# A four-layer kernel on one core: the next batch's gated-attention front moved to a round's end, score and one-hot products issued by row groups in turn, and two residual sums made on TensorE

## What is computed

```
x = layernorm(x + gated_attention(x))        # "a": silu(normed @ W_h) gives v and gate, groups of 32 tokens
                                             #      quad_out + lin_out, times gate, @ W_out + b_out + x
x = layernorm(x + experts(x))                # "a": softmax of 8 logits, top 2 of 8 experts
x = layernorm(x + linear_attention(x))       # "b": 16 heads of 8, softmax feature maps, causal sums
x = layernorm(x + product_keys(x))           # "peer": 8 heads; per head the best 8 of 32 + 32 keys, the best 8 sums,
                                             #      those rows of down and up:
    hmid = sigmoid(score) * gelu(x . down[index]);  out = sum(hmid * up[index])
```

## Time and profile before

| | |
|---|---|
| median of 3 runs | 570.6 us |
| the profiled execution | 572.47 us |
| its span, first to last instruction | 570.7 us |
| mean granted TensorE clock | 0.733 of full speed |
| busy: PE, PE weight loads, DVE, ACT, GpSimd (POOL) | 419.4, 300.4, 481.5, 307.2, 182.2 us |
| layers, peer | 0 to 314.3 us, 314.3 to 570.7 us |

### The profile page before, as it was taken

How to read it: one execution, slowest core, us unless ns; L and a number is a source line. 1 busy time by engine, 2 the same in 40 slices (tenths; PEclk the granted TensorE clock), 3 DMA queues, 4 the chain that set the end, 5 groups by cost and what they waited for, 6 DMA issues and landing times. The chain is left out here.

```text
span 570.7 us, 12499 instructions
## 1 busy us (share of the span) xinstructions
PE 419.4 (73%) x4564; PEld 300.4 (53%) x4564; DVE 481.5 (84%) x2076; ACT 307.2 (54%) x639; POOL 182.2 (32%) x208
## 2 busy tenths in 40 slices
PE   1777869987999879965754864756698869784485
PEld 1454547654776457633653323554465555554475
DVE  4485877699887989599894699999999999999991
ACT  0611275426652475313640558483788778786591
POOL 4540122943277143833350330303040404030000
PEclk9997979688867977795555785575757575757577
DMA  7220000000000000000000000000000000000000
GB/s 214 71 59 0 1 2 2 1 2 0 1 1 3 0 2 1 2 1 0 1 2 1 1 1 1 3 1 11 2 11 1 12 2 12 1 11 2 11 2 20
DMA packets 12459, 6.72 MB, mean 12 GB/s; under 512 B 3182, under 2 KB 11758, under 8 KB 12398
## 3 DMA queue, kind: packets, MB, share of 16 engines
q1 hardware_dynamic: 10566, 4.34, 2.8%
q10 hardware_dynamic: 1832, 1.58, 0.9%
HBM read 4.87 MB, written 1.05 MB: 10 GB/s over the span
## 5 line engine op out<-in xcount | busy, mean ns | idle before, releaser
L1746 ACT ACTIVATE hot_last<-iota_f,lo_last 128x128 f16<-128x128 f32 x256 | 77.5, 393 | 0.3 <-DVE lo_last L1872 0.3
L2015 PE MATMUL psum<-hot_w,hot_lo 128*128 128x16 f16 x1536 | 44.3, 174 | 25.1 <-DVE hot_lo L1889 17.9
L2015 PEld LDWEIGHTS psum<-hot_w,hot_lo 128*128 128x128 f16 x1536 | 43.4, 104 | 36.8 <-DVE hot_lo L1889 24.5
L1979 PE MATMUL psum<-x3t,down_t 128*128 128x512 f32 x64 | 45.3, 832 | 16.8 <-ACT hid L1711 15.1
L1889 DVE TENSOR_TENSOR hot_lo<-lo_t,iota_lo 128x4096 f16<-128x4096 f16 x24 | 53.6, 2287 | 0.3
L1659 POOL TENSOR_TENSOR eq<-eq,side_f 128x1024 f16<-128x1024 f16 x14 | 28.9, 2085 | 55.9 <-DVE eq L1850 55.9
L1329 PE MATMUL psum<-q_hi,k_t 32*128 32x128 f16 x256 | 36.1, 259 | 8.9 <-DVE masked L905 7.7
L1667 POOL TENSOR_TENSOR rstd<-rstd,minus_half 128x2 f32<-128x2 f32 x8 | 5.6, 702 | 113.4 <-DVE rstd L1922 113.4
L1819 DVE FIND_INDEX8 side_i<-side,keysims 128x8 uint32<-128x32 f32 x256 | 41.5, 184 | 0.0
L1250 PE MATMUL psum<-we,x1t 128*128 128x512 f32 x64 | 40.2, 777 | 0.4 <-DVE z L842 0.4
L2029 PE MATMUL psum<-upw,mix 128*128 128x128 f32 x256 | 36.9, 306 | 0.0
(11 more groups left out here) (271 smaller groups left out, 1166.8 us busy)
## 6 DMA issues: line engine op xcount, KB each, us to landing
xall<-in_L_attn_x SPq DMA_DIRECT2D x4, 256.0 KB, 6.3
out<-o SPq DMA_DIRECT2D x8, 128.0 KB, 2.3
we<-in_L_ffn_We SPq DMA_DIRECT2D x1, 512.0 KB, 4.4
downn<-in_L_ffn_down SPq DMA_DIRECT2D x1, 512.0 KB, 5.3
upw<-in_L_ffn_up SPq DMA_DIRECT2D x1, 512.0 KB, 6.3
wh<-in_L_attn_W_h SPq DMA_DIRECT2D x1, 256.0 KB, 4.7
keysn<-in_L_ffn_keys_p ACTq DMA_DIRECT2D x1, 256.0 KB, 9.7
wqkv<-in_L_attn_w_qkv ACTq DMA_DIRECT2D x1, 192.0 KB
```

The source lines that it names most:

```text
L1746: ins = nc.scalar.activation(hot_last[:, lane], iota_f[:], ACT.Abs, bias=lo_last[:, lane:lane + 1], scale=-1.0)
L1979: nc.tensor.matmul(bank[H_BANK(b, c)][:], v.down_t[:, c, :], v.x3t[:, N * b:N * b + N], start=True, stop=True).then_inc(h_mm.h, 1)
L2015: ins = nc.tensor.matmul(bank[2 + q][:, c:c + 2 * EH], low, hot_w[:, i, lane // 2, :, :, lane % 2].rearrange("p t e -> p (t e)"), start=(i ...
```

## The change

- `a_qk`, `a_gate`, `a_val` of batch a + 1 are issued at the end of round s on PE, and their Silus there on ACT (`a_front`), in the order qk, gate 0, val 0, val 1, gate 1 (`a_rest` is the last four on PE); batch 1's before round 1. The steps behind them stand elsewhere in the round.
- `b_scores` issues the products of the groups in turn (as many groups as there are banks) and waits once for all of their banks. In rounds 1 to 3 `a_experts(a, 1)` is cut in two between scores.
- `a_z` and `b_z3` on DVE are gone: PE adds the residual to the same PSUM columns as a product with the identity, and mean, variance and normalising read PSUM.
- POOL no longer waits for x1 before the low parts of the scores.
- `hot_w` loses the zero halves: each tile of the pair is a product on its own 64 rows, 8 columns, into a bank of its own; two tiles in turn. `weigh` waits for two quarters at a time. The division by `WEIGHT_SCALE` moves from `weigh` into `upw`, once, on POOL; the memset of `hot_w` is gone.
- `key_scores(0)` is issued before `hidden(0, 1)`.

```
-                for s in range(1, B + 1):
+                a_qk(1)
+                a_rest(1)
+                for s in range(1, B + 1):
...
                 for u in range(T):
                     for c in range(EC):
-                        ins = nc.tensor.matmul(bank[3]..., gated_t, v.wout0, start=(c == 0), stop=(c == EC - 1))
+                        nc.tensor.matmul(bank[3]..., gated_t, v.wout0, start=(c == 0), stop=False)
+                    if u == 0:
+                        wait(pe, xres_ok, b)
+                    ins = nc.tensor.matmul(bank[3]..., ident[:], v.xall[:, T * b + u, :], start=False, stop=True)
...
-                    b_scores(b, 0)
+                    b_scores(b, 0, (0,))
+                    b_scores(b, 0, (1,))
...
                         a_experts(a, 0)
-                        a_experts(a, 1)
                         b_scores(b, 2, (1,))
+                        a_experts(a, 1, (0,))
                         b_scores(b, 3, (0,))
+                        a_experts(a, 1, (1,))
+                        b_scores(b, 3, (1,))
                         b_numerators(b, 1)
-                        b_scores(b, 3, (1,))
...
+                    b_yt(b)
+                    if a + 1 < B:
+                        a_qk(a + 1)
                     b_z3(b)
+                    if a + 1 < B:
+                        a_rest(a + 1)
...
-                    for t in range(2):
-                        q = slice(HK * t, HK * t + HK)
-                        for i, w in enumerate((w_hi, w_lo)):
-                            ins = nc.vector.tensor_tensor(hot_w[q, i, :, t], hot_hi[q], bc(w[q]...), ALU.mult)
+                    for i, w in enumerate((w_hi, w_lo)):
+                        ins = nc.vector.tensor_tensor(hot_w[:, i], hot_hi[:], bc(w[:]...), ALU.mult)
...
                     for lane in range(LB * q, LB * q + LB):
                         for i in range(2):
-                            ins = nc.tensor.matmul(bank[2 + q][:, c:c + 2 * EH], low, hot_w[:, i, lane // 2, :, :, lane % 2], ...)
+                            for t in range(2):
+                                half, c = slice(HK * t, HK * t + HK), EH * (lane % (2 * LB))
+                                low = hot_lo[half, lane // 2, :, lane % 2] if q < QB - 1 else hot_last[half, lane - LB * q, :]
+                                ins = nc.tensor.matmul(bank[2 + q // 2 * 2 + t][:, c:c + EH], low, hot_w[half, i, lane // 2, :, lane % 2], ...)
...
                 hidden(0, 0)
+                key_scores(0)
                 hidden(0, 1)
-                key_scores(0)
```

More of the change, by code:

```diff
@@ L531, in _ @@
                 act.wait_ge(pads.h, 2)
+                a_front(1)
                 for s in range(1, B + 1):
@@ L1050, in _ @@
                 a_gated(0, 1)
-                a_z(0)
                 a_z_spread(0)
@@ L1129, in _ @@
                         b_y(b)
-                b_z3(B - 1)
                 b_z3_spread(B - 1)
@@ L1248, in a_experts @@
                         wait(pe, y_used, b, 1)
-                    for k in range(2):
+                    for k in halves:
                         ins = nc.tensor.matmul(bank[Y_BANK[u] + k][:], x1t[:, P * u:P * u + P],
@@ L1321, in b_scores @@
                         wait(pe, qlo_ok, b, 3)
-                    for g in (2 * i + j for i in halves for j in range(2)):
-                        banks = len(set(S_BANK[b]))
-                        if 4 * u + g >= banks:
-                            wait(pe, masked_ok, b, 4 * u + g - banks + 1)
-                        r = slice(32 * g, 32 * g + 32)
+                    banks = len(set(S_BANK[b]))
+                    groups = [2 * i + j for i in halves for j in range(2)]
+                    for first in range(0, len(groups), banks):
+                        together = groups[first:first + banks]
+                        if 4 * u + together[-1] >= banks:
+                            wait(pe, masked_ok, b, 4 * u + together[-1] - banks + 1)
                         for c in range(QUADS):
                             for q in (q_hi, q_lo):
-                                ins = nc.tensor.matmul(bank[S_BANK[b][g]][:, P * c:P * c + P], k_t[r, u, c, :],
-                                                       q[r, u, c, :], start=(q is q_hi), stop=(q is q_lo))
-                        ins.then_inc(a_mm.h, 1)
+                                for g in together:
+                                    r = slice(32 * g, 32 * g + 32)
+                                    ins = nc.tensor.matmul(bank[S_BANK[b][g]][:, P * c:P * c + P], k_t[r, u, c, :],
+                                                           q[r, u, c, :], start=(q is q_hi), stop=(q is q_lo))
+                                    if c == QUADS - 1 and q is q_lo:
+                                        ins.then_inc(a_mm.h, 1)
                 def b_numerators(b, u):
@@ L1366, in b_numerators, with b_yt @@
                     ins.then_inc(num_mm.h, 1)
-                def b_z3(b):
+                def b_yt(b):
                     wait(pe, y_ok, b)
```

172 lines of the change are left out of this document (85 added, 87 removed).

## The result

The changed kernel takes 582.0 us (median of 4 runs, 580.85 to 584.49) against 570.9 us: 1.0187 times the time before, 95% interval 1.0161 to 1.0214, so it is slower by 1.9%. (The 570.6 us given ahead of the prediction were the median of three of the four runs before.) The profiled execution has a span of 581.1 us against 570.7.

The account below looks back on a forecast made before the run. In the pairs the time was taken as the sum of DVE's instructions; in the rounds' score parts DVE waits for PE. Rounds -2.3, between the blocks +0.3, pairs -7.7 gave -9.7: 560.9 us from 570.6, range 553 to 574.

Parts of the forecast that it names:

- the rest of `layers` +0.6 with `key_scores(0)`: Outside the rounds: +0.3 us for later masking in batch 0, +0.3 between the blocks including the earlier `key_scores(0)`.
- pairs -8.3: Seven pairs: two fewer `hot_w` instructions on DVE save 9.0 us, a stall in pair 2 costs 0.7.
- last pair +0.6: Last pair: the fourth quarter waits for ACT, so nothing is saved; two `mix` stand behind it instead of one, +0.6 us.
- Where a stall goes: Pairs: `weigh` waits by twos, so DVE waits 0.6 to 0.7 us before pair 2's third `mix`; other pairs free.
- I take 1.9 us, unchanged: PE's gather: a quarter's 128 products of 8 columns, two row groups side by side, take 1.9 us as before.
- Rival (2): Gather: each small product in turn at 29 ns, 3.5 to 3.7 us a quarter, 30 to 46 lost: 590 to 607; chance 0.18.
- Front, round 2 and its neighbours: Rounds' first parts: DVE waits 2.8 us for ACT's exponential; round 2 +1.7, rounds 1 and 3 +0.3 each, round 4 -0.7.
- I add nothing for POOL's earlier start.: Low scores on POOL without the wait for x1: no gain counted, since its root of the variance stands ahead.
- Masking +1.8: Query part (`a_out`): 16 PE instructions become 24, so masking starts 0.85 or 0.55 us later, three times: +1.8 us.
- Middle, -6.0: Part with the last scores, rounds 1 to 3: half the expert products ahead, groups in turn; -2.0, -1.6, -2.4 us.
- Between the blocks: Between `layers` and pairs: identity products less the dropped addition +1.4 us, `key_scores(0)` 1.1 earlier, together +0.3.

Follow-up runs that it names:

- one_part: Changed kernel with the gather's products with w_lo left out, 64 products a quarter instead of 128 (output loses the weights' low part): 572.2 us, 1.001.
- exp_and_parts: Changed kernel, ScalarE's front Silus behind the round's first exponential, GpSimd's two subtractions made to wait for DVE's k and attn_t: 571.7 us, 0.999.
- no_wait_only: Kernel before without GpSimd's wait for x1, and nothing else: 582.2 us, 1.0178.
- identity_only: Kernel before with only the two residual sums as products with the identity; means, variances and normalising read PSUM: 579.6 us, 1.0136.
- middle_wait: Kernel before with scores in turn and expert products cut in two between them, GpSimd's wait for x1 kept: 568.9 us, 0.996.
- peer_new: Kernel before with only the change's part in `peer`; `layers` as before: 570.9 us, 0.9981.
- middle_and_peer: Kernel before with scores in turn, expert products cut in two, GpSimd's wait kept, and the new `peer`: 567.7 us, 0.9935.
- again_three: Changed kernel plus three stretches of 768 small products behind its last: two row groups in turn, one row group, all 128 rows: 643.5 us, one run.

## Why the prediction was wrong, by its steps

The forecast was 560.9 us with a range of 553 to 574; 582.0 lies outside. By the table its sum of -9.7 was made of: rounds' first parts +1.6, mask +1.8, scores and sums -6.0, the rest of `layers` +0.6 with `key_scores(0)`, pairs -8.3, last pair +0.6. Measured: +10.8, +2.0, -3.8, -0.4, -1.7, +3.6, together +10.3 in the profiled spans (the parts are rounded).

- **"Where a stall goes" and "I take 1.9 us, unchanged" (pairs).** This step failed: a term of -7.7 us that came out at +1.9. `hot_w` gave what was said: DVE is 9.1 us less busy, and the pairs of one_part are 9.9 us shorter than before. The two row groups ran side by side as argued, 1.87 us for 128 products. But a quarter that needs a block not yet fetched lasts longer by about 1.6 us per block. DVE waited 7.7 us for the gather in the seven pairs, where the forecast had 0.7, and 3.5 us more than before in the last. The last pair grew by 3.6 in all: 2.1 up to PE's output products, and 1.5 because these ran at a granted clock of 0.58, as in kernels whose `peer` is that of before. The price missing from the sum was one per instruction, not per product, column or row. Rival (2) had the sentence for it ("something other than columns sets the pace") and its place, but a price of 30 to 46 us; one_part puts it at 9.8.
- **Front, round 2 and its neighbours.** This step failed too, a term of +1.6 that came out at +10.8. The wait before the sums was right, 2.93 us for 2.8 forecast, and so was its cause. What failed is the rest of the step: rounds 1 and 3 got +0.3, because waits that they had before were to vanish. They did not. DVE's idle time in the first part rose by 2.5, 2.9 and 1.7 us in rounds 1, 2, 3 (length less busy time in the stretches after, against the earlier trace rows and, for round 1 before, 20.12 us with 14.36 busy), and DVE's busy time by 1.4, 1.0 and 1.0, which the forecast did not have at all: `k` and `attn_t` beside GpSimd. exp_and_parts shows that these two are the front's loss.
- **"I add nothing for POOL's earlier start."** Right in the changed kernel, but only because x1 is read from PSUM there. no_wait_only shows the price of that line by itself: 10 us. The residual sums on PE are what made it free.
- **Masking +1.8.** The parts between the first `q_lo` and `wexp` are 1.0, 0.5 and 0.5 us longer: right in size and place. The whole of identity_only, 7.2 us in the median, is not: in the profiled execution 3.6, of which the clock explains 1.4 in the last pair and most of the 2.4 in the part with the last scores, and the rest is open.
- **Middle, -6.0.** The mechanism was right, the size was off: -3.8 in the changed kernel, -4.7 in middle_wait. DVE's wait for tile 2's second half is 2.4, 2.15 and 1.9 us in rounds 1 to 3 and not 1.3. In round 2 the four expert instructions (two fp32 products) ahead of it ran at a granted clock of 0.50, which is 1.2 GHz, 3.76 us for four:

```profile
174.85:178.61 3.76, 3.76 (x13) 1.22 (x11) 2.27 (x9) 1.80 (x3) 3.76 (x4) 0.50 0.02 4
```

  Eight took 5.25 us in the row on which the step rested, so half of that was 2.6.
- **Between the blocks.** `key_scores(0)` brought 0.4 us or less (peer_new, and nothing in middle_and_peer against middle_wait), not 1.1.

Still open: the part of identity_only's time that its trace does not show. And whether the 1.5 us that the granted clock cost in the last pair of the changed kernel's trace stand in its median too is not shown, since only one execution of each kernel has a trace.

## What to carry to other kernels

When an edit multiplies instructions, price the instructions as well as the work: look for gaps ended by "issue" at a fixed count, and count PE's instructions between its rests, since what was fetched ahead while PE rested or did longer work is free, and what comes after it is paid by the block. When an edit moves a step on one engine, list what follows it on GpSimd and what DVE does at that moment; two instructions that never met before can hold each other. And a wait that seems to order nothing may be what keeps them apart: try its removal by itself.

## What the hardware showed that was not expected

- PE's instructions come in blocks of 256, each in some 3.45 us inside the pairs and in 3.46 to 3.75 us in a long stretch, with some two blocks there ahead (257 products without a gap behind a rest in again_three). The Trainium skill, page "Runtime: NRT & Kernel Launch", section "Instruction fetch mechanics", gives PE a store of 2048 instructions; no run here shows more than some 512 ahead.
- Two products on two row groups of 64 rows take 14.6 ns each in turn, on one row group 27 ns and on all 128 rows 27 to 28 ns, all at a granted clock of 0.50.
- GpSimd holds some DVE instructions until its own is done: `k` goes from 0.41 to 1.42 us, `attn_t` from 0.69 to 1.64, x1 from SBUF from 0.28 to 1.12 us a tile. It does not hold x1 from PSUM: the four instructions take 1.36 us in all (0.34 a tile) beside GpSimd's `s_lo`, and 1.36 as well in batch 0, where GpSimd does nothing. The Trainium skill, page "SBUF — State Buffer", section "Who interferes with whom", has the rule: DVE instructions in a two-port mode, or with both inputs in SBUF against a GpSimd instruction that reads SBUF, share a port with it, and the other blocks; an instruction with at most one input in SBUF, outside those modes, does not. All four rows agree with it; `k` and `attn_t` have both inputs in SBUF. That x1 from SBUF, with one input, runs in such a mode is the page's account; the trace shows only that it was held.
